# Gated block, four batches: where the second batch pair's rows are normed, turned and kept, and the order of the up signs

## The reference

```python
def layernorm(x): return (x - mean(x)) / sqrt(var(x) + 1e-5)

# cross attention, per batch; keys and values: the context rows, then the projected new rows
n = layernorm(x)
q, k_new, v_new = n @ wq.T, n @ wk.T, n @ wv.T
k, v = concat(ctx, k_new), concat(ctx, v_new)          # 1024 keys
x = x + tanh(g_xattn) * (softmax(q @ k.T / sqrt(512)) @ v) @ wo.T

# feed-forward with the signs of its weights; 2048 hidden features
h = relu((layernorm(x) @ sign(up).T) * up_scale)
x = x + tanh(g_ffn) * ((h @ sign(down).T) * down_scale) * output_scale
```

## Time and profile before

| | us |
|---|---|
| median of three runs | 618.79 |
| the profiled execution's own time | 619.17 |
| its span in the profile | 617.4 |
| TensorE (PE) busy | 600.1 (97%) |
| VectorE (DVE) busy | 300.3 (49%) |
| ScalarE (ACT) busy | 242.4 (39%) |
| GpSimd (POOL) busy | 124.9 (20%) |
| granted TensorE clock, mean | 0.999 |

### The profile page before, as it was taken

How to read it: one execution, slowest core, us unless ns; L and a number is a source line. 1 busy time by engine, 2 the same in 40 slices (tenths; PEclk the granted TensorE clock), 3 DMA queues, 4 the chain that set the end, 5 groups by cost and what they waited for, 6 DMA issues and landing times.

```text
span 617.4 us, 6921 instructions
## 1 busy us (share of the span) xinstructions
PE 600.1 (97%) x2786; PEld 496.1 (80%) x2786; DVE 300.3 (49%) x443; ACT 242.4 (39%) x362; POOL 124.9 (20%) x116
## 2 busy tenths in 40 slices
PE   8999999999999999999999998999998899999997
PEld 6888888888888888888887786788886687888885
DVE  4335622225622235522237264655565865676564
ACT  3724311224321225220237444556465535556531
POOL 5750202000202002102002105232331003242002
PEclk9999999999999999999999999999999999999999
DMA  8750304000303000303022123121211002231011
GB/s 297 269 184 18 104 1 136 1 0 1 102 1 136 1 1 0 103 0 103 1 58 79 36 63 108 35 68 35 68 35 34 2 0 68 68 113 59 2 70 68
DMA packets 19808, 39.00 MB, mean 63 GB/s; under 512 B 4800, under 2 KB 4800, under 8 KB 19648
## 3 DMA queue, kind: packets, MB, share of 16 engines
q1 hardware_dynamic: 19776, 38.56, 18.8%
HBM read 34.35 MB, written 4.21 MB: 62 GB/s over the span
## 4 chain that ended last, share of the span: by engine, by line
PE 88%; DVE 5%; DMA 3%; ACT 2%; issue 1%; SPq 0%; ACTq 0%
PE proj L420 31%; PE score L420 20%; PE score L496 17%; PE turn L481 12%; PE proj L481 4%; PE turn L412 2%; DMA raw_w<-in_ffn_w 2%; PE score L622 2%; DMA rows<-in_x 1%; DVE hid_split L1179 1%; PE turn L473 1%; DVE raw_x L1042 1%; DVE ops_a L1050 1%; ACT down_signs L735 1%; DVE raw_x L1064 0%
## 5 line engine op out<-in xcount | busy, mean ns | idle before, releaser
L496 PE MATMUL score<-down_signs,hid_split 128*128 128x512 f32 x512 | 135.3, 391 | 6.2 <-DVE hid_split L1179 5.7
L496 PEld LDWEIGHTS score<-down_signs,hid_split 128*128 128x128 f32 x512 | 95.3, 188 | 28.2 <-DVE hid_split L1179 7.9
L715 ACT ACTIVATE four_x<-proj 128x512 fp32r<-128x512 f32 x60 | 35.8, 598 | 163.3 <-PE proj L420 163.3
L420 PE MATMUL score<-four_x 128*128 128x512 f32 x384 | 89.9, 391 | 0.0
L420 PE MATMUL proj<-probsT,four_x 128*128 128x512 f32 x384 | 88.1, 390 | 0.0
L420 PEld LDWEIGHTS proj<-probsT,four_x 128*128 128x128 f32 x384 | 71.9, 188 | 14.9
L420 PEld LDWEIGHTS score<-four_x 128*128 128x128 f32 x384 | 71.5, 188 | 14.6
L420 PE MATMUL proj<-four_x,weights 128*128 128x512 f32 x336 | 76.8, 389 | 0.0
L956 DVE TENSOR_TENSOR four_x<-proj,four_x 128x512 fp32r<-128x512 f32 x44 | 30.3, 690 | 94.8 <-ACT four_x L715 94.8
L420 PEld LDWEIGHTS proj<-four_x,weights 128*128 128x128 f32 x336 | 63.0, 188 | 13.0
L347 POOL TENSOR_TENSOR four_x<-raw_ctx,four_x 128x2048 fp32r<-128x2048 f32 x8 | 36.9, 4611 | 116.5 <-ACT four_x L707 116.5
(11 more groups left out here) (96 smaller groups left out, 641.2 us busy)
## 6 DMA issues: line engine op xcount, KB each, us to landing
raw_w<-in_ffn_w SPq DMA_DIRECT2D x24, 512.0 KB, 3.3
raw_ctx<-in_ctx_turned SPq DMA_DIRECT2D x4, 1024.0 KB, 6.0
raw_ctx<-in_ctx SPq DMA_DIRECT2D x4, 1024.0 KB, 5.4
result<-rows SPq DMA_DIRECT2D x16, 256.0 KB, 2.0
rows<-in_x SPq DMA_DIRECT2D x3, 1024.0 KB, 5.7
turned_x<-in_x_turned SPq DMA_DIRECT2D x3, 1024.0 KB, 7.9
all_facts<-row_facts SPq DMA_DIRECT2D x3, 512.0 KB, 5.2
rows<-in_x SPq DMA_DIRECT2D x4, 256.0 KB, 4.5
```

The costliest lines, as they stand in the source:

```text
L420: last = pe.matmul(bank, lhs(l), rhs(r), start=start and i == 0, stop=stop and i == 2)
L496: last = pe.matmul(wide(r), hid_split[:, n % HR, s, r * P:(r + 1) * P], down_signs[:, chunk_of(q), :], start=(q == 0 and s == HI), stop=(q ...
L715: act.activation(dst, proj_bank(n), ACT.Copy, scale=scale).then_inc(proj_hi, 1)
```

## The change

- `raw_x[1]` moves from 184 KB to 0, over the first eight row tiles of `rows` (batches 0 and 1). These are written to a DRAM tensor `rows_away` by one DMA of 2 MB in batch 2, right behind the `all_facts` load for batch 3, and read back by one DMA of 2 MB once pair 1's operands are made; `add_rows` of batches 0 and 1 waits for it.
- The eight row tiles of pair 1 are turned inside the groups 1, 2, 5 and 6, two per group, one after piece 1 and one after piece 2, in the half of `proj` that the group does not use. ScalarE copies all eight. Their statistics and norms move earlier on VectorE (from the last batch to group 4), the inverse deviations on GpSimd likewise.
- T3 and T1 of pair 1 are made after groups 6 and 7; T3 and T2 have a place of their own (`normed`).
- In the last batch the rows of pair 0 are turned two at a time, after jobs m+2, m+3, m+4 and m+5; VectorE's statistics for them come later than before.
- The sign tile up 0 comes before down 7, and takes 5, 6, 7 stand earlier. Up 0 may be taken once the last batch's new values are read (`new_read`), where before it stood behind job m+7.
- In group 0 the first hidden tile is split once half of the out pieces are done (`half_out`), not after all.

```diff
-        raw_x = [at("raw_x0", 192, [P, 2, DC, ROWS]), at("raw_x1", 184, [P, 2, DC, ROWS])]
+        raw_x = [at("raw_x0", 192, [P, 2, DC, ROWS]), at("raw_x1", 0, [P, 2, DC, ROWS])]
+        SIGNS = [("down", i) for i in range(HG - 1)] + [("up", 0), ("down", HG - 1)] + [
+            ("up", g) for g in range(1, 2 * HG)]
+        TURNED_IN = {1: 2 * RT, 2: 2 * RT + 2, 5: 3 * RT, 6: 3 * RT + 2}
+        SUM_ORDER = ((T1, T3, T2, T4), (T3, T1, T2, T4))
...
+                if b + 2 == BATCH:
+                    sp.wait_ge(attended, 2 * RT)
+                    sp.dma_start(rows_away, rows[:, 0:2 * RT, :]).then_inc(rows_spilled, 16)
...
-            for n in range(HG + 13):
+            for n in range(HG + 11):
+                load_signs(n)
+            sp.wait_ge(rows_spilled, 16)
+            sp.wait_ge(x_ready, x_at(1, T4))
+            sp.dma_start(rows[:, 0:2 * RT, :], rows_away).then_inc(rows_back, 16)
+            for n in range(HG + 11, HG + 13):
                 load_signs(n)
...
+            inverse_std(BATCH + 2)
...
-                if g == 5:
-                    inverse_std(BATCH + 2)
-                if g == 8:
+                if g == 4:
                     inverse_std(BATCH + 3)
...
+                if pair == 0 and j - 1 in TURNED_IN:
+                    pe.wait_ge(raw_out, TURNED_IN[j - 1] + 2)
...
                 piece(1)
+                if pair == 0 and j in TURNED_IN:
+                    pe.wait_ge(relu_done, 4 * (g - 1) + 1)
+                    turn_block_rows(TURNED_IN[j], proj[:, (g + 1) % 2, :])
...
                 piece(2)
+                if pair == 0 and j in TURNED_IN:
+                    pe.wait_ge(raw_out, TURNED_IN[j] + 1)
+                    turn_block_rows(TURNED_IN[j] + 1, proj[:, (g + 1) % 2, :])
...
                 proj_job(n + 2, v_terms(2))
+                if last_batch:
+                    turn_two(0)
                 proj_job(n + 3, v_terms(3))
                 if last_batch:
-                    for f in range(RT):
-                        turn_block_rows(f)
+                    turn_two(2)
...
-                    if last_batch and e == 0:
-                        for f in range(RT, 2 * RT):
-                            turn_block_rows(f)
+                    if last_batch and e < 2:
+                        turn_two(RT + 2 * e)
...
-                if q == 0:
-                    pe.wait_ge(up_sums, sum_done(HG - 1, AT_C12))
-                if q < 4:
-                    turn_block_rows(2 * RT + 2 * q)
-                    turn_block_rows(2 * RT + 2 * q + 1)
...
                 act.activation(p1_copy, proj[:, g % 2, :], ACT.Copy).then_inc(p1_out, 1)
+                if pair == 0 and j in TURNED_IN:
+                    act.wait_ge(rows_spilled, 16)
+                    block_rows_out(TURNED_IN[j], proj[:, (g + 1) % 2, :])
+                    block_rows_out(TURNED_IN[j] + 1, proj[:, (g + 1) % 2, :])
...
-                if g > 0:
-                    hidden_high(2 * pair, 2 * j)
+                if g == 0:
+                    act.wait_ge(half_out, 1)
+                hidden_high(2 * pair, 2 * j)
...
             for q in range(2, HC - 2):
                 hidden_high(1, q)
-                if q in (2, 3):
...
-                    block_rows_out(2 * RT + 2 * q - 4)
-                    block_rows_out(2 * RT + 2 * q - 3)
-                if 4 <= q < 11:
-                    right_high(1, (B11, B21, B22, T1, T3, T2, T4)[q - 4])
+                if q < 9:
+                    right_high(1, X_ORDER[q - 2])
...
-                if q in (2, 3):
-                    block_rows_out(3 * RT + 2 * q - 4)
-                    block_rows_out(3 * RT + 2 * q - 3)
...
+                if q == 2:
+                    right_low(1, B11)
                 if q == 3:
-                    right_low(1, B11)
+                    right_sum(1, T2)
...
                 if q == 10:
-                    right_sum(1, T4)
-                if q == 11:
-                    right_low(1, T3)
-                if q == 12:
-                    right_low(1, T2)
-                if q == 13:
                     right_low(1, T4)
```

More of the change, by code:

```diff
@@ L236, in load_signs @@
                     sp.wait_ge(signs_ready, n)
-                sp.dma_start(raw_w[:, :], ffn_w[n if n < HC else n - HG]).then_inc(signs_in, 16)
+                kind, i = SIGNS[n]
+                sp.dma_start(raw_w[:, :], ffn_w[i if kind == "down" else HG + i % HG]).then_inc(signs_in, 16)
             def store(t):
@@ L460, in turn_probs, with turn_block_rows @@
                     turn_job(turn0(b) + 2 * t + half, cols(probs[:, t % 2, half * 512:(half + 1) * 512]))
-            def turn_block_rows(f):
+            def turn_block_rows(f, bank):
                 pe.wait_ge(normed_done, RT + f + 1)
[L465 to L471, removed]
                 for k, tile in enumerate(cols(normed[:, f % RT, :])):
@@ L474, in turn_block_rows, with turn_two @@
                 last.then_inc(turned, 1)
+            def turn_two(f):
+                for i in (f, f + 1):
+                    if i < 2:
+                        pe.wait_ge(turn_lo, TURNS_ALL + i - 1)
+                    else:
+                        pe.wait_ge(raw_out, i - 1)
+                    turn_block_rows(i, turn[:, i % 2, :])
             def up_product(g, k, bank, left, i, start, stop):
@@ L521, in up_group @@
                 if j == 0:
[L522 to L524 removed]
+                    pe.wait_ge(raw_out, 2 * RT + 2 * RT * pair)
                     pe.wait_ge(x_ready, x_at(pair, T3))
@@ L578, in batch @@
                             pe.wait_ge(proj_lo, n + i + 1)
-                        product(proj[:, e % 2, :], lhs, rhs, i == 0, False)
+                        last = product(proj[:, e % 2, :], lhs, rhs, i == 0, False)
+                    if last_batch and e == DC - 1:
+                        last.then_inc(new_read, 1)
                     if e == 0:
@@ L598, in out_piece @@
                         last.then_inc(wo_done, 1)
+                    elif last_batch and c == 1 and r == RT - 1:
+                        last.then_inc(half_out, 1)
                 for i in range(2 * RT if last_batch else DC * RT):
@@ L727, in take_signs @@
                 act.wait_ge(signs_in, 16 * (n + 1))
-                if n < HG:
-                    dst = down_signs[:, 2 * n:2 * n + 2, :].rearrange("p j n -> p (j n)")
-                else:
[L731 to L734, removed]
+                kind, i = SIGNS[n]
+                if kind == "down":
+                    dst = down_signs[:, 2 * i:2 * i + 2, :].rearrange("p j n -> p (j n)")
+                else:
+                    dst = up_ops[:, i % 2, A11:A22 + 1, :].rearrange("p k n -> p (k n)")
+                    if i == 0:
+                        act.wait_ge(new_read, 1)
+                    if i >= 2:
+                        act.wait_ge(up_done, 7 * (i - 1))
@@ L735, in take_signs, with block_rows_out @@
                 act.activation(dst, raw_w[:, :], ACT.Sign).then_inc(signs_ready, 1)
-            def block_rows_out(f):
+            def block_rows_out(f, bank):
                 act.wait_ge(turned, TURNS_ALL + f + 1)
-                act.activation(raw_x[f // (2 * RT)][:, f // RT % 2, :, f % RT * P:(f % RT + 1) * P],
-                               four(turn_bank(TURNS_ALL + f)), ACT.Copy).then_inc(raw_out, 1)
+                act.activation(raw_x[f // (2 * RT)][:, f // RT % 2, :, f % RT * P:(f % RT + 1) * P], four(bank), ACT.Copy
+                               ).then_inc(raw_out, 1)
@@ L743, in right_high, with two_rows_out @@
+            def two_rows_out(f):
+                for i in (f, f + 1):
+                    block_rows_out(i, turn[:, i % 2, :])
             def right_high(pair, i):
[L744 to L747, removed]
                 if i in (B11, B21):
@@ L749, in right_high @@
                     act.wait_ge(raw_out, 2 * RT * pair + RT)
-                elif i == B22 and pair == 0:
-                    act.wait_ge(raw_out, 2 * RT)
                 elif i == B22:
-                    act.wait_ge(raw_by_vector, RT)
+                    act.wait_ge(raw_out, 2 * RT * pair + 2 * RT)
                 else:
-                    act.wait_ge(x_sums, 4 * pair + (T1, T3, T2, T4).index(i) + 1)
+                    act.wait_ge(x_sums, summed(pair, i))
                 if pair == 1:
@@ L757, in right_high @@
                     act.wait_ge(up_done, product_done(HG - 1, AT_P3))
-                act.activation(right(i)[:, HI], src, ACT.Copy).then_inc(x_hi, 1)
+                act.activation(right(i)[:, HI], right_raw(pair, i), ACT.Copy).then_inc(x_hi, 1)
             def rows_out(n, r, dst):
@@ L1059, in attend @@
                                          ).then_inc(attended, 1)
-            def block_rows_out(f):
-                dve.wait_ge(turned, TURNS_ALL + f + 1)
-                dve.tensor_copy(raw_x[1][:, 1, :, f % RT * P:(f % RT + 1) * P], four(turn_bank(TURNS_ALL + f))
-                                ).then_inc(raw_by_vector, 1)
```

(3 more changed lines are left out.)

115 lines of the change are left out of this document (62 added, 53 removed).

## The result

Four runs of the changed kernel gave 608.29 to 608.82 us, median 608.44; before, four runs gave a median of 618.84. The ratio is 0.9824 (95% interval 0.9800 to 0.9848). The forecast was 608.4.

A forecast was written before the change was run, and what follows sets the result against it. TensorE, busy 600.1 of 617.4 us, was taken as the bound, so only its waits could go. Gains 4.81 + 5.95 - 0.35 = 10.4 us gave a median of 608.4 us, range 606.8 to 612.3.

The forecast's parts named there:

- five terms of the last batch and group 0: Job m+2 to group 1's first down product: waits removed, 0.27 + 1.25 + 1.31 + 1.28 + 0.70 = 4.81 us.
- term 1: Ahead of job m+2 in the last batch: TensorE's 0.53 us wait for VectorE's low part shrinks; gain 0.27 us.
- The stage: Stage of batch 1, first turning block to group 8: all 5.95 us of TensorE's waits go.
- The switches: Matmul-to-transpose switches in the groups and last batch: six more than before, cost 0 to 0.7 us, taken as 0.35.
- The lower end of the range: Whole kernel: 606.8 us, if the switches are free and part 1 gives all.
- part 1: Same as term 1: the wait ahead of job m+2, gain between 0 and 0.53 us, taken as 0.27.
- rival B: Turned tiles stall four groups, waiting for ScalarE's copy: 2.4 to 4.8 us lost, 610.7 to 613; chance 0.10.
- rival D: Whole kernel: removed waits return for something taken as hidden; less than 3 us stay, 616 to 618; chance 0.03.
- rival C: Batch 2: spill delays the facts, one us per us beyond 3.9; chance 0.03 partial (609.9), 0.02 slower than before.

The follow-up runs named there:

- e1: Changed kernel with the sign tiles in the old order (up 0 ninth) and taken at the old, late places; 610.72 us.
- e5: Changed kernel with pair 0's rows turned four at a time again, behind jobs m+3 and m+4; 609.52 us.
- e6: Changed kernel with the first hidden tile split behind all out pieces again; 609.10 us.
- e9: Kernel before, with ScalarE instead of VectorE copying the last four row tiles of pair 1 in the stage of batch 1; 614.98 us.
- e10: Changed kernel with pair 1's operands made at their old places in the stage of batch 1, rows still turned in the groups; 608.59 us.
- e7: Changed kernel with the 2 MB spill issued ahead of batch 3's facts instead of behind them, and done twice; 616.50 us.
- e8: Changed kernel with only one of the four transposes of each of pair 1's eight row tiles; 606.20 us.
- e4: Changed kernel with e1, e5 and e6 together, pair 1's rows still turned in the groups; 612.97 us.

## Why the prediction was right

- Each of the five terms of the last batch and group 0 was read as a distance between two starts less the matmuls between them, and came out within 0.03 us in the table; e1, e5 and e6 gave 2.58, 1.1 and 0.70 back when undone, for 2.6, 1.25 and 0.70. The half that I took of term 1 (0.27 of 0.53) was a middle between bounds, and that it came out exact is luck; no run undoes term 1 alone.
- The stage: its 5.95 us of waits are gone, as forecast. The cause that I named, copies that wait in VectorE's queue, is shown by e9 for 3.6 us. Of the rest, 1.1 us came from ScalarE's operands behind the turned rows, and 1.2 from the exchange of T4 between the two engines, which my account of the 5.95 us did not set apart: e9 keeps both, and e10, with the rows turned early and the operands at their old places, has neither on TensorE. So turning in the stage was what let them reach TensorE.
- The switches were the term that was mis-sized. From group 1's first down to group 8 the gain is 10.77 - 4.83 = 5.94 us, forecast 5.95 - 0.35 = 5.6. The eight tiles cost the groups 3.75 us (0.47 each), where 3.62 had been taken out of the stage: that is 0.13 for the four switches more, and no 0.35 (the two switches in the last batch are inside its five terms). Another 0.16 us is a loss of the kernel before that I had not counted: behind the wait at 391.48 its group 1 needs 9.24 us to the start of group 2, at 400.72, for 40 matmuls or 9.08.
- The trace gained 10.8 us and the medians 10.4. That the median is within 0.1 us of the forecast is therefore luck in part: the profiled execution before stood 0.4 us above its median and the one after did not.
- The lower end of the range does not follow from its own conditions: switches free (0.35) and all of part 1 (0.26 more) make 607.8 and not 606.8. The measured time lies inside either.
- Against rival B: no tile waited in a group; the second was turned 1.83 us after the first, which is its six matmuls and one tile. Against rival D: the gain is 10.77 us at group 8 and 10.8 at the end, so nothing was handed on.
- The sum for rival C was sound in its slack and its price per us, but incomplete: it left out the clock.

## What to carry to other kernels

Where one engine is busy 97% of the span, take its pace from one long run, then subtract: distances between starts less the work between them sum up to the gain of a reordering, to a few tenths of a microsecond. An in-order engine that waits for one hand-over holds all that is queued behind it; moving that wait to where nothing urgent follows is worth more than its own work (four copies of 0.68 held 3.6 us). When two edits shorten the same chain, undo each alone before calling both needed. A large transfer belongs behind the small one that something waits for.

## What the runs showed of the hardware that I had not expected

After TensorE had stood idle from 265.7 us in e7, its granted clock fell to 0.50 at 268.7, 1.2 and not 2.4 GHz, and stayed there until 275.5. For the last 5.3 us of this TensorE was at work, and the next 48 matmuls took 13.49 us (270.20 to 283.69) where 10.89 is their time at full pace. So the gap cost 4.5 us and 2.6 more.

The length of one gap does not tell whether this happens. The waits of up to 2.7 us in the stage of batch 1 before the change are followed by no such drop: none of that trace's first 600 microseconds is under 0.98. But e7 has an earlier stretch at 0.50 too, and e8 and e9 have one: each is 3.4 us long and lies between 11.4 and 16.1 us. It begins soon after TensorE waited 2.42, 1.54 and 1.65 us for an operand that ScalarE splits, behind small matmuls. The traces of e4 and e5 have 1.52 and 1.79 us of idle time at the same place, and no drop behind it. In e9:

```profile
10.18 1.21 PE L618 MATMUL score<-four_x,weights 128*128 128x256 f32 x8 [1.65 <-ACT four_x L707]
```
```profile
12.00:14.00 2.00, 2.00 (x11) 2.00 (x11) 1.43 (x5) 0.00 (x0) 0.79 (x1) 0.50 1.02 384
```

The changed kernel has 19 matmuls in these two microseconds, e9 has 11. This is part of why later starts shift between traces, and no part of what the change did.
